# The order of the first group's work, and the residual reads and weighted sums of the last stage, in an adaLN block with a 16-expert mixture

## The reference

```python
mod = (_silu(L0_c) @ L0_wmod).reshape(L0_c.shape[0], 6, 1, -1)
sa, ca, ga, sb, cb, gb = (mod[:, 0], mod[:, 1], mod[:, 2], mod[:, 3], mod[:, 4], mod[:, 5])
...
h = _layernorm(x, axis=-1) * (1 + ca) + sa
x = x + ga * _L0_attn_ref(h, L0_attn_W_qkv, L0_attn_W_o)
h = _layernorm(x, axis=-1) * (1 + cb) + sb
x = x + gb * _L0_ffn_ref(h, L0_ffn_Wg, L0_ffn_balance_bias, L0_ffn_W1, L0_ffn_W2)
```

## Time and profile before

| | |
|---|---|
| runs | 1644.54, 1652.25, 1651.16 us |
| median | 1651.16 us |
| profiled execution, its own time | 1648.23 us |
| its span | 1645.6 us |
| PE busy | 1410.0 us, 86% |
| DVE busy | 1252.1 us, 76% |
| ACT busy | 792.3 us, 48% |
| POOL busy | 733.0 us, 45% |

### The profile page before, as it was taken

One profiled execution on the slowest core, in us unless ns is written; L12 is line 12 of the kernel. 1 busy time (PEld: TensorE's weight loads), 2 busy tenths in 40 slices (PEclk: granted clock), 3 DMA queues, 4 the chain that ended last, 5 costly groups with the idle time before them and its releaser, 6 DMA issues. The chain is left out here.

```text
span 1645.6 us, 27981 instructions
## 1 busy us (share of the span) xinstructions
PE 1410.0 (86%) x8713; PEld 1006.4 (61%) x8713; DVE 1252.1 (76%) x2928; ACT 792.3 (48%) x1414; POOL 733.0 (45%) x683
## 2 busy tenths in 40 slices
PE   4679998899999889999988999999973999999900
PEld 3557665566566566656655666665441999999800
DVE  3578787787778778777867877789757777777778
ACT  4324546634354663334456434445513666666622
POOL 3244355342435434243543333364425677777500
PEclk8899999999999999999999999999995999999955
DMA  6555564445355444535534453553744455445389
GB/s 220 170 162 155 153 164 112 117 123 155 104 152 159 119 117 123 156 104 143 155 104 130 131 156 91 130 138 83 279 150 167 160 185 185 142 147 172 117 327 371
DMA packets 141491, 256.14 MB, mean 156 GB/s; under 512 B 17200, under 2 KB 81200, under 8 KB 141376
## 3 DMA queue, kind: packets, MB, share of 16 engines
q1 hardware_dynamic: 113280, 178.70, 36.9%
q0 software_dynamic: 13792, 47.72, 8.6%
q10 hardware_dynamic: 14304, 28.32, 5.1%
HBM read 167.34 MB, written 85.75 MB: 154 GB/s over the span
## 5 line engine op out<-in xcount | busy, mean ns | idle before, releaser
L682 ACT ACTIVATE probs<-ring 128x1024 f32<-128x1024 f32 (+3 forms) x384 | 310.8, 812 | 188.5 <-PE ring L536 116.0
L501 PE MATMUL ring<-stack_t 96*128 96x512 f32 (+3 forms) x768 | 295.6, 409 | 18.8 <-DMA stack_t<-stack_dram 15.6
L479 PE MATMUL ring<-w_parts,h_hi 128*128 128x384 f32 x1024 | 277.0, 352 | 9.8 <-DVE neg_max L863 4.0
L866 DVE CUSTOM_DVE_ANT_0 ring<-ring,later_b 128x384 f32<-128x384 f32 (+3 forms) x512 | 247.9, 497 | 26.1 <-PE ring L501 25.1
L501 PEld LDWEIGHTS ring<-stack_t 96*128 96x128 f32 x768 | 141.1, 192 | 169.9 <-issue 61.5
L1150 POOL TENSOR_TENSOR prob_sum<-prob_sum,probs 128x1024 f32<-128x1024 f32 (+3 forms) x128 | 230.0, 1797 | 29.1 <-ACT probs L682 28.5
L1163 POOL TENSOR_TENSOR rope_a<-rope_a,rope_b 128x256 f32<-128x256 f32 x128 | 93.4, 730 | 334.6 <-DVE rope_b L936 334.5
L530 PE MATMUL ring<-stack_t 128*128 128x512 f32 (+3 forms) x768 | 210.6, 356 | 26.1 <-ACT probs L682 17.2
L479 PEld LDWEIGHTS ring<-w_parts,h_hi 128*128 128x128 f32 x1024 | 190.9, 198 | 20.0 <-issue 13.2
L863 DVE TENSOR_REDUCE neg_max<-ring 128x1 f32<-128x512 f32 x256 | 175.0, 684 | 17.1 <-PE ring L501 14.8
L479 PE MATMUL ring<-w_parts,h_lo 128*128 128x384 f32 x512 | 177.4, 346 | 0.0
(11 more groups left out here) (192 smaller groups left out, 2385.6 us busy)
## 6 DMA issues: line engine op xcount, KB each, us to landing
stack_t<-stack_dram SPq DMA_DIRECT2D x384, 128.0 KB, 3.3
stack_dram<-parts SPq DMA_DIRECT2D x64, 512.0 KB, 2.9
w_parts<-w_dram SPq DMA_DIRECT2D x96, 192.0 KB, 3.5
w_sb<-y_dram SPq DMA_DIRECT2D x32, 512.0 KB, 6.6
w_sb<-w SPq DMA_DIRECT2D x22, 512.0 KB, 5.7
x_in<-x SPq DMA_DIRECT2D x32, 256.0 KB, 3.7
x<-x SPq DMA_DIRECT2D x32, 256.0 KB, 3.7
x_dram<-x SPq DMA_DIRECT2D x32, 256.0 KB, 2.9
```

The lines of the kernel that those rows point to most:

```text
L479: mm = nc.tensor.matmul(ring[:, BANK[use], 0:384], lhs[:, c, cols], rhs[:, c, :], start=(k == 0), stop=(k == len(products) - 1))
L501: nc.tensor.matmul(ring[:, BANK[use], 0:width], stack_t[0:MROW, i % 2, 0, h, qt * P:qt * P + P], stack_t[0:MROW, i % 2, 1, h, kc * 512:kc ...
L682: nc.scalar.activation(probs[:, step % PROBS, :, q0:QC], ring[:, bank:bank + 2, q0:QC], ACT.Exp)\
L866: nc.vector.tensor_tensor_reduce(ring[:, BANK[use], 0:width], ring[:, BANK[use], 0:width], later_b[:, QC - width:QC], -1.0, 3e38, ALU.add, ...
```

## The change

The diff has three parts.

1. **Group 0's order.** Its projections move two steps ahead (2t-32), so the statistics, normalisations, transposes and turns move with them, while the score rows stay at step -23 and on. In a step, group 0's turn now stands behind the projection on PE, ACT and DVE; ACT normalises a tile one step sooner, ahead of `values_of`; the split of the first weights moves two further steps ahead, before the first statistics; DVE takes the second tile's statistics between the two modulation copies. ACT issues the load of the first weights behind its first activation instead of ahead of all else; SP issues the second x tile ahead of the constants. POOL's two memsets move to the kernel's very start.
2. **Group 1's turns** run three steps behind their projections instead of two.
3. **The last stage.** Twelve more residual tiles (32 in all) are read in the expert part, over the weights of the experts 2 to 4, when `w2_lo_r` is 66, 67 and 68; the last stage reads none. For ten of the 32 tiles (2, 5, ..., 29) ACT scales both results, PE sums them with two float32 matmuls against the identity into `sum_ps`, and DVE starts with the product with gb. ACT issues the output of tile t-3 instead of t-2.

```diff
 def project_step(i, t):
-    return STEPS * (i - 1) + 3 * t - 13 if i else 2 * t - 30
+    return STEPS * (i - 1) + 3 * t - 13 if i else 2 * t - 32
...
-TURN = {step + 2: it for step, it in PROJECT.items()}
+TURN = {step + (3 if it[0] == 1 else 2): it for step, it in PROJECT.items()}
...
-SPLIT = {MOD_COL: 0, -20: 1, 3: 2, 26: 3}
+SPLIT = {MOD_COL - 2: 0, -20: 1, 3: 2, 26: 3}
...
-                        if step == FIRST_STEP + 1:
+                        if step == FIRST_STEP + 3:
                             for dst, src in ((trig[:, :, :, :, :], rope), (mask_f, mask), (k_ones_sb[:, :], k_ones),
...
-                        if step in TURN:
+                        if step in TURN and TURN[step][0]:
                             turn(*TURN[step])
...
                         if step in PROJECT:
                             project(*PROJECT[step])
+                        if step in TURN and TURN[step][0] == 0:
+                            turn(*TURN[step])
...
-                    load_raw_w(0)
                     nc.scalar.preload_act_table_set("natural_log_exp_and_others")
                     act.wait_ge(c_in, 16)
                     nc.scalar.activation(c_exp[:, :, :], c_sb[:, :, :], ACT.Exp, scale=-1.0).then_inc(silu_step, 1)
+                    load_raw_w(0)
...
+                        if step + 1 in NORM_B and NORM_B[step + 1][0] == 0:
+                            normalise(*NORM_B[step + 1])
                         if step in PROJECT:
                             values_of(*PROJECT[step])
+                        if step in TURN and TURN[step][0] == 0:
+                            high_parts(*TURN[step])
...
                         if step == MOD_COL:
                             modulation_parts(SA)
+                            statistics(*NORM_A[step])
                             modulation_parts(CA)
...
-            EARLY, FREED = 12, 8
+            EARLY, FREED = 12, TT - 12
             most = -(-B * L // P)
+            past = [most * (e + 1) if e < 2 else 2 * most + e for e in range(FREED // 4)]
...
-                            sp.wait_ge(w2_lo_r, most * ((t - EARLY) // 4 + 1))
+                            sp.wait_ge(w2_lo_r, past[(t - EARLY) // 4])
...
+            BY_PE = [t for t in range(2, TT - 2) if t % 3 == 2]
...
+                        pe.wait_ge(m_a, n + 1)
+                        pe.wait_ge(m_b, t + 1)
+                        if n >= 2:
+                            pe.wait_ge(m_g, BY_PE[n - 2] + 1)
+                        for half in range(2):
+                            mm = nc.tensor.matmul(sum_ps[:, n % 2, :], ident_f[:, :], y_pair[:, t % DEPTH, half, :],
+                                                  start=(half == 0), stop=(half == 1))
+                        mm.then_inc(m_s, 1)
...
+                            if t in nth:
+                                nc.scalar.activation(y_pair[:, k, 0, :], y_pair[:, k, 0, :], ACT.Copy, scale=weight[:, t, 0:1])\
+                                    .then_inc(m_a, 1)
...
+                        if t in nth:
+                            dve.wait_ge(m_s, nth[t] + 1)
+                            summed_y = sum_ps[:, nth[t] % 2, :]
```

More of the change, by code:

```diff
@@ L95 @@
 MOD_ROWS = -10
-FIXED = {-28 + 3 * n: (0, n) for n in range(1 + HG)} | {-8 + n: (1, n) for n in range(1 + HG)}
+FIXED = {-28 + 3 * n: (0, n) for n in range(HG)} | {-8 + n: (1, n) for n in range(HG)}
 TIMELINE = range(FIRST_STEP, LAST_STEP + 1)
@@ L117, in uses_of @@
                         ("second_t", SECOND_T), ("logits", SECOND_L)):
-        if step in table:
+        if step in table and not (kind == "turn" and table[step][0] == 0):
             major, minor = table[step]
@@ L124, in uses_of @@
         uses.append(("project", NT * PROJECT[step][0] + PROJECT[step][1]))
+    if step in TURN and TURN[step][0] == 0:
+        uses.append(("turn", TURN[step][1]))
     return uses
@@ L812, in _ @@
                             exponentials(step)
-                        if step in NORM_B:
+                        if step in NORM_B and NORM_B[step][0]:
                             normalise(*NORM_B[step])
@@ L1084, in _ @@
                             parts_of_shift(*MAX_COMBINE[step])
-                        if step in NORM_A:
+                        if step in NORM_A and step != MOD_COL:
                             statistics(*NORM_A[step])
@@ L1104, in _ @@
                             rope(*PROJECT[step])
+                        if step in TURN and TURN[step][0] == 0:
+                            low_parts(*TURN[step])
                         if step >= EARLY_GATE:
@@ L1432, in adaln_block @@
             w2_tiles = w2_sb[:, :, :, :].rearrange("p e f d -> p (e f) d")
-            x_early += [tiles[:, 2 * e + n, :] for e in range(2) for tiles in (w1_tiles, w2_tiles) for n in range(2)]
+            x_early += [tiles[:, 2 * e + n, :] for e in range(FREED // 4) for tiles in (w1_tiles, w2_tiles) for n in range(2)]
             early_in = sem("early_in")
```

55 lines of the change are left out of this document (28 added, 27 removed).

## The result

| | before | changed |
|---|---|---|
| median of 20 runs each | 1652.03 us (1644.54 to 1655.97) | 1657.55 us (1651.66 to 1659.88) |
| ratio, 95% interval | 1 | 1.0031 (1.0021 to 1.0041) |
| profiled execution, span | 1648.2, 1645.6 | 1656.9, 1654.9 |
| first score columns of step 0 | 109.7 | 110.3 |
| parts of set 8 go out | 153.96 | 159.22 |

What follows compares the result with a forecast made beforehand. PE is busy except at both ends; waits on `stack_t`, `x_hat` and turns hold the start, DVE then transfers the last stage. Start 12.5 us plus last stage 8: 1651.2 - 20.5 = 1631 us, range 1645 to 1620.

Steps and rivals of the forecast that it cites:

- The first projection: Start: with the split taken out from between, it begins at about 21 us instead of 22.85.
- The pace of a tile: Start, group 0: a tile takes 3.9 us, from ACT's 3.55 us of work, instead of 4.57 us.
- Set 2: Start: its parts go out at 55 and are back at 66.5 us instead of 74.98, a gain of 8.5 us.
- The first rival: Start: it stays tied to `stack_t`, only 3 to 4 us of the first part remain; 1639 us, chance 0.15.
- From step -15 to step 0: Start, second part: half of the 7.8 us of waits on the rope sum is saved, 4 us, bounds 0 and 7.8.
- The late pieces of group 1: Start: pieces come four steps ahead of their use instead of five at the tightest place, costing nothing, at most 1 us.
- The expert part: Expert part: three bursts of residual reads on end cost nothing, at most 4 us.
- The last stage: Last stage: 64 us instead of 71.2, a gain of 8 us with the shorter tail, bounds 2 and 11.
- The second rival: Last stage: the ring of eight buffers holds it at 2.26 us a tile, 72 us, no gain; 1640 us, chance 0.13.
- The slower rival: Last stage: the same ring at late-stretch times, 2.71 us a tile, 87 us; 1663 or 1655 us in all, chance 0.05.
- The rule: Last stage: HBM binds at about 358 GB/s, so 70 us and 3 us less gain; set aside for the trace's 412.
- the fourth case: Both ends: both holds apply, the start gives 4 us and the last stage nothing; 1647 us, chance 0.07.

Runs made afterwards that it cites:

- e8: e5 with DVE's low half of the first weights behind the modulation columns again; ratio to the kernel before 0.9998.
- e5: Kernel before with only the changed start, but group 1's turns two steps behind their projections as before; ratio to the kernel before 1.0013.
- e2: Kernel before with only the changed expert part and last stage, eight pair buffers; ratio to the kernel before 1.0030.
- e6: Kernel before with one edit, group 1's turns three steps behind their projections instead of two; ratio 0.9998.
- e11: e2 with a tile's output issued two tiles behind ACT instead of three; ratio to the kernel before 1.0029.
- e9: e5 with the statistics of group 0 a step earlier, ahead of the rotation on DVE; ratio to the kernel before 1.0015.
- e7: e5 with the second pair of modulation weights, the modulation rows and group 2's raw weights loaded later; ratio to the kernel before 0.9984.
- e4: e2 with twelve pair buffers in the last stage instead of eight; ratio to the kernel before 0.9953, and 0.9953 when run again.
- e10: e3 with twelve pair buffers in the last stage instead of eight; ratio to the kernel before 0.9991.
- e13: e9 with both pairs of modulation weights loaded at steps -15 and -14, rows at -6, group 2's raw weights at -12; ratio to the kernel before 1.0007.
- e3: Kernel before with only the twelve residual reads moved into the expert part, no sums on PE, eight buffers; ratio 0.9975.

## Why the prediction was wrong

Forecast 1631 us, 20 us faster; measured 5 us slower. By its own steps:

**The first projection** was put at 21 us, bounds 20.9 and 24.4; it came at 24.75. The step that failed is "the split is taken out from between": DVE's 1.76 us went from one place on the way to the first projection to another, ahead of the two copies for the modulation columns, with the statistics behind it. Only the row of the split was costed, not what now stands behind it on its engine. That is 1.9 us of the 3.75: e8, with this operation behind the columns again, begins the first projection at 23.16 against 25.07 in e5. Of the rest the traces show two parts. The first tile's statistics begin at 13.26 us in e8, when x has landed, against 12.10 before. And the sixteen small matmuls that sum the columns take 3.57 us in the changed kernel, where before has

```profile
13.75 1.95 PE L619 MATMUL ring<-add_up,mod_b 128*128 128x4 f32 x16 [0.66 <-DVE mod_b L1028]
```

They take the longer time in every trace with the changed start, and also in e2, e6 and e11, which have the old one. Neither part was in the prediction, and no run isolates them; the granted clock is recorded as 1.00 in both, and what makes the sums slow stays open.

**The pace of a tile**, 3.9 us by ACT's own work, was 4.6. ACT's 3.55 us are right, as e9's 3.6 shows; what was missed is that the reordering made ACT's next normalisation wait for DVE work that waits for ACT. A sum over one engine gives a bound, and the loop through ACT, DVE and POOL was the longer.

**PE's behaviour at sets 0 and 1** was right: one wait at set 0, of 3.7 us, and none at set 1.

**Set 2** was to go out at 55, cost 9.9 + 1.5 us and be used at 66.5. It went out at 60.48 and took 16.1. The 1.5 us for the 2 MB was the undersized term; it was 4.7 more. Of these 6.2 us over the 9.9, 4.4 lie in the write (7.5 us to landing against 3.1 before) and 1.8 in the pieces (8.6 against 6.8), beside which ACT has asked for the raw weights of group 2, 768 KB, at 68.10; the prediction does not count these. In e7 the 2 MB meet set 3's write instead, which takes 8.1 us against 3.2 before. The 5.5 us on the way to 60.48 are in the main the two points above. The first rival, a start tied to `stack_t`, describes this, though it left 4 us of gain where nothing was left.

**From step -15 to step 0** half of 7.8 us was to be saved; PE's waits for the turns fell by 5.1 us, a wait of 1.4 for `neg_max` came in their place, as forecast of DVE, and the way took 33.7 us instead of 34.7. Here the mechanism held and 1 us came of it.

**The late pieces of group 1**, "nothing, at most 1 us", are a wait of 2.5 us and more in all five traces with the late turns. The slack in steps was counted, but not that the weights are written in just these steps.

**The expert part** was right. PE in the changed kernel, with three bursts of reads from 1515 us on:

```profile
1515.00:1525.00 10.00, 10.00 (x75) 9.21 (x73) 7.80 (x12) 7.18 (x12) 7.21 (x6) 1.00 0.83 261
1525.00:1535.00 10.00, 10.00 (x76) 9.27 (x75) 7.94 (x12) 6.38 (x11) 7.15 (x6) 1.00 0.96 337
```

**The last stage** was to take 64 us. Its terms were right: DVE's 60 us, 3.75 us for a sum at the lower clock (3.6 forecast), one wait of 3 us at the first; e4 has them all, at 63.2. What failed is "these times are those of a full queue and shrink when fewer transfers are open", with which the ring was put aside. They hardly shrank: from 6.0 + 5.4 to 5.3 + 5.1 us between 1594 and 1614 us, and not at all between 1620 and 1640, where they are 6.2 + 5.2. In a round of 8 x 2.28 = 18.2 us that leaves 7.8 and 6.8 us for all that lies between landing and output, against the rival's 6.7. The second rival's T of 2.26 us was the measured one, to 1%. It had a chance of 0.13; the sum of the round was on the page and deserved more than the argument against it. The slower rival (87 us) did not come: the times to landing stayed near 6 and 5 us.

**The rule.** By the Trainium skill, DMA: Bandwidth & Descriptors, section Bandwidth, the HBM side binds at about 358 GB/s; e4 moved 409 and e10 415 GB/s for 40 us. That agrees with what the Trainium skill says in HBM Reference, section Specifications (TRN2), that a core streaming alone measures about 425, and this kernel runs on one core alone. The prediction's estimate from the first page, a gain 3 us smaller than its own, is worked out wrongly: 70 us are 6 more than its 64, and nearly the whole gain.

Both ends failing together, the fourth case, had 0.07 and 1647 us. Its two reasons, the start tied to `stack_t` and the ring, are the ones found; that both would also lose a little was in none. So what failed is mechanism and not only size: at the start the order of work on DVE and ACT and the loads beside set 2, at the end the argument against the ring.

## What to carry to other kernels

Before taking a stage's bound from the busiest engine, write down the round that a buffer makes (load, each engine, output, load) and divide by the number of buffers; if that is above the bound, work taken off the engine gains nothing and a longer way for it loses. When an operation is moved on one engine, look at what now stands behind it there, and follow that until it comes back to the moved one: a loop sets the pace whatever the sums say. A large load placed beside a chain of smaller transfers delays the chain, here one write by 4 to 5 us for 2 MB; move it in the table of the queue that issues it and read when it is issued, because that engine may be far ahead of the step's name.

## What the runs showed of the hardware

- A write of 0.5 MB, 2.7 us to landing for set 1 of the changed kernel, took 6.6 to 8.3 us when 2 to 4 MB of loads had been issued up to 5.5 us ahead of it, on another queue: set 0 in e9, set 2 in the changed kernel, set 3 in e7 and e13.
- Loads and outputs side by side kept 409 to 415 GB/s for 40 us in e4 and e10, at times to landing of 5.9 us for a load and 6.7 for an output in e4, 7.1 and 5.9 in e10; with eight buffers, as in e2, e3 and e11, the same queues gave 330 to 376 GB/s at 5.8 to 6.1 and 5.2 to 5.5 us. In e3 that is what DVE, the bound there, asks for.
- Two float32 matmuls of 128x512 with nothing else on PE took 3.75 us at a granted clock of 0.50 in most of the ten sums, and 1.96 us in two of e4's, at 1.00.
